# Perceiver cross attention: value products computed transposed, two heads side by side in column halves, then turned back

## What is computed

```
x = x + cross_attention(context, layernorm(x), mask)   # this case's stage
x = x + causal_attention(layernorm(x), Qw, Kw, Vw)
x = x + two_layers_of(local attention + gated FFN)(layernorm(x))

# cross_attention, 16 heads of 64; 4 batches; 256 latents; context of 4096 tokens of width 256
xn, ln_lat = layer_norm(context), layer_norm(latents)
q = ln_lat @ Wq
k, v = split(concat([xn, ln_lat]) @ Wkv)
weight = where(mask, (q * s) @ (k * s).T, -max)        # s = 64 ** -0.25
out = softmax(weight) @ v ; result = out @ Wout
```

## Time and profile before

| | before |
|---|---|
| median of 3 runs | 1054.46 us (1053.11 to 1055.18) |
| the profiled execution | 1054.65 us |
| span from its first to its last instruction | 1052.8 us |
| granted TensorE clock, mean | 0.995 of 2.4 GHz |
| PE / PEld / DVE / ACT / POOL busy | 1014.3 / 943.1 / 809.3 / 666.8 / 204.1 us |

### The profile page before, as it was taken

How to read it: one execution, slowest core, us unless ns; L and a number is a source line. 1 busy time by engine, 2 the same in 40 slices (tenths; PEclk the granted TensorE clock), 3 DMA queues, 4 the chain that set the end, 5 groups by cost and what they waited for, 6 DMA issues and landing times. The chain is left out here.

```text
span 1052.8 us, 25657 instructions
## 1 busy us (share of the span) xinstructions
PE 1014.3 (96%) x8683; PEld 943.1 (90%) x8684; DVE 809.3 (77%) x3001; ACT 666.8 (63%) x1550; POOL 204.1 (19%) x265
## 2 busy tenths in 40 slices
PE   6999999999999999999999998988999999999997
PEld 6899999999999999999999998977888999889887
DVE  7887777685877786787787777579879889889753
ACT  4765565674665665566565566478776876767753
POOL 0111111110111111111111111342015203263213
PEclk9999999999999999999999999999999999999999
DMA  6000000000000000000000100520010000110000
GB/s 208 18 13 2 10 1 1 12 12 4 12 2 0 12 13 3 13 2 0 12 13 2 35 2 2 166 38 2 1 41 21 2 1 21 35 48 2 1 22 21
DMA packets 28803, 21.64 MB, mean 21 GB/s; under 512 B 12094, under 2 KB 26267, under 8 KB 28699
## 3 DMA queue, kind: packets, MB, share of 16 engines
q1 hardware_dynamic: 28529, 20.21, 6.5%
q10 hardware_dynamic: 170, 0.07, 0.0%
HBM read 19.17 MB, written 1.05 MB: 19 GB/s over the span
## 5 line engine op out<-in xcount | busy, mean ns | idle before, releaser
L303 PEld LDWEIGHTS pv_ps<-v,pt 128*128 128x128 f32 x1792 | 214.9, 192 | 9.3 <-issue 2.8
L303 PE MATMUL pv_ps<-v,pt 128*128 128x65 f32 x1792 | 215.2, 272 | 3.2 <-DVE o L818 1.8
L796 DVE CUSTOM_DVE_ANT_0 s_sb<-s_ps,pen,mstate 128x256 f32<-128x256 f32 (+1 forms) x512 | 199.9, 446 | 13.9 <-issue 11.0
L510 ACT ACTIVATE probs<-s_sb,mbias 128x256 f32<-128x256 f32 (+1 forms) x512 | 203.2, 470 | 0.0
L670 POOL TENSOR_TENSOR o<-o,alpha 128x260 f32<-128x260 f32 x128 | 85.7, 669 | 561.3 <-ACT alpha L504 561.3
L519 ACT ACTIVATE pt<-turn 128x512 f32<-128x512 f32 x128 | 76.2, 595 | 123.0 <-PE turn L290 109.1
L290 PE MATMUL turn<-ident,probs 128*128 128x128 f32 x896 | 123.8, 278 | 0.1
L290 PEld LDWEIGHTS turn<-ident,probs 128*128 128x128 f32 x896 | 98.8, 145 | 9.5 <-issue 0.3
L818 DVE TENSOR_TENSOR o<-o,pv_ps 128x260 f32<-128x260 f32 x128 | 53.9, 421 | 46.1 <-PE pv_ps L303 34.7
L279 PE MATMUL s_ps<-kh,qh 64*128 64x256 f32 (+1 forms) x512 | 78.9, 304 | 2.9 <-DVE x L840 1.6
L768 DVE TENSOR_TENSOR kl<-proj,kh 128x512 fp32r<-128x512 f32 (+1 forms) x63 | 41.3, 655 | 51.5 <-ACT kh L497 51.0
(11 more groups left out here) (432 smaller groups left out, 2730.7 us busy)
## 6 DMA issues: line engine op xcount, KB each, us to landing
raw<-in_ctx SPq DMA_DIRECT2D x24, 128.0 KB, 2.0
f_wqkv_raw<-in_L_ffn_wqkv SPq DMA_DIRECT2D x6, 512.0 KB, 5.3
f_w_raw<-in_L_ffn_w SPq DMA_DIRECT2D x8, 256.0 KB, 5.1
f_w_raw<-in_L_ffn_w SPq DMA_DIRECT2D x2, 640.0 KB
wkv_raw<-in_L_xattn_Wkv SPq DMA_DIRECT2D x1, 1024.0 KB, 8.5
wout_raw<-in_L_xattn_Wout SPq DMA_DIRECT2D x1, 1024.0 KB, 12.5
f_wo_raw<-in_L_ffn_wo SPq DMA_DIRECT2D x2, 512.0 KB, 4.7
x<-in_x SPq DMA_DIRECT2D x1, 768.0 KB, 9.6
```

The source lines that it names most:

```text
L303: last = pe.matmul(t.pv_ps[:, u, :], t.pt[g % 2][:, u, kt, :], t.v[:, kt, h, :], start=(kt == 0), stop=(kt == kts - 1))
L510: last = act.activation(t.probs[g % 2][:, u, 0:kts * P], t.s_sb[g % 2][:, u, 0:kts * P], ACT.Exp, bias=t.mbias[:, at:at + 1], scale=0.125)
L796: last = dve.tensor_tensor_reduce(out=t.s_sb[g % 2][:, u, 0:width], in0=t.s_ps[g % 2][:, u, 0:width], in1=t.pen[:, 0:width], scale=1.0, sc ...
```

## The change

`weighted_values` swaps its operands: a head's values (128 keys by 64) are the weights, and the turned probabilities of both query tiles (256 columns) stream past. The first head of a group writes PSUM partitions 0 to 63, the second 64 to 127. The result is the transposed output; it goes into parts of `s_ps[0]`, is copied by ACT (`store_outputs`) into `ov`, turned back on PE (`turn_back`) into `pv_ps`, and added by DVE. Since there is no column of ones any more, the exponentials give their row sums (`accum_out`), and POOL adds them to the denominator. All of it happens for two groups at a time, at odd steps: the products behind the probabilities' transposes (ahead of them in `finish` steps), the turning back behind the projection (directly behind the transposes in `finish` steps).

```diff
+    def pair_at(m, kind, prev, j):
+        return [now for now in (at_step(m, kind, prev, j - 4), at_step(m, kind, prev, j - 3)) if now] if j % 2 else []
+    def output_bank(g):
+        return t.s_ps[0][:, 2 - g % 2 * 2, :]
...
 def weighted_values(m, g, kts):
-                if g or not isinstance(m, int):
-                    pe.wait_ge(s["o_added"], 8 * m + g)
-                for u in range(GU):
-                    h = 2 * g + u // QT
-                    for kt in range(kts):
-                        last = pe.matmul(t.pv_ps[:, u, :], t.pt[g % 2][:, u, kt, :], t.v[:, kt, h, :],
+                for kt in range(kts):
+                    for o, rows in enumerate((slice(0, DH), slice(DH, P))):
+                        last = pe.matmul(output_bank(g)[rows, :], t.v[:, kt, 2 * g + o, :], t.pt[g % 2][:, QT * o:QT * o + QT, kt, :],
                                          start=(kt == 0), stop=(kt == kts - 1))
                 last.then_inc(s["pv_done"], 1)
+            def turn_back(pair):
+                for m, g, kts in pair:
+                    pe.wait_ge(s["ov_stored"], 8 * m + g + 1)
+                first_m, first_g, _ = pair[0]
+                if first_g or not isinstance(first_m, int):
+                    pe.wait_ge(s["o_added"], 8 * first_m + first_g)
+                for m, g, kts in pair:
+                    for qt in range(QT):
+                        last = pe.transpose(t.pv_ps[:, 1 - g % 2, qt * P:(qt + 1) * P], t.ov[g % 2][:, qt * P:(qt + 1) * P], t.ident[:])
+                last.then_inc(s["o_turned_back"], len(pair))
...
 PE body
+                    pair = pair_at(m, kind, prev, j)
+                    if pair and finish:
+                        pe.wait_ge(s["s_read"], 8 * m + (j + 2 if kind else 2))
+                        for now in pair:
+                            weighted_values(*now)
                     now = at_step(m, kind, prev, j - 2)
                     if now:
                         turn_probs(*now)
+                    if pair and not finish:
+                        pe.wait_ge(s["s_read"], 8 * m + (j + 2 if kind else 2))
+                        for now in pair:
+                            weighted_values(*now)
+                    if pair and finish:
+                        turn_back(pair)
...
-                    now = at_step(m, kind, prev, j - 3)
-                    if now:
-                        weighted_values(*now)
+                    if pair and not finish:
+                        turn_back(pair)
...
 ACT
-                                          bias=t.mbias[:, at:at + 1], scale=0.125)
+                                          bias=t.mbias[:, at:at + 1], scale=0.125, accum_out=t.sums[:, at:at + 1])
+            def store_outputs(m, g, kts):
+                act.wait_ge(s["pv_done"], 8 * m + g + 1)
+                if g >= 2 or not isinstance(m, int):
+                    act.wait_ge(s["o_turned_back"], 8 * m + g - 1)
+                act.activation(t.ov[g % 2][:], output_bank(g), ACT.Copy).then_inc(s["ov_stored"], 1)
 ACT body
                 for j in range(NG if kind else 6):
+                    for now in pair_at(m, kind, prev, j):
+                        store_outputs(*now)
...
 POOL body, behind the rescaling of o
+                    pool.wait_ge(s["rescaled"], 16 * m + 2 * g + 1)
+                    pool.wait_ge(s["p_ready"], 8 * m + g + 1)
+                    pool.tensor_tensor(t.o[:, cols, DH], t.o[:, cols, DH], t.sums[:, cols], ALU.add).then_inc(s["rescaled"], 1)
...
 DVE add_output
-                dve.wait_ge(s["pv_done"], 8 * m + g + 1)
-                dve.tensor_tensor(t.o[:, cols, :], t.o[:, cols, :], t.pv_ps[:], ALU.add).then_inc(s["o_added"], 1)
+                added = t.o[:, cols, 0:DH].rearrange("p (o q) d -> p o q d", q=QT)
+                dve.tensor_tensor(added, added, t.pv_ps[:, 1 - g % 2, :].rearrange("p (q o d) -> p o q d", q=QT, o=2), ALU.add
+                                  ).then_inc(s["o_added"], 1)
 DVE body
-                    now = at_step(m, kind, prev, j - 4)
-                    if now:
-                        add_output(*now)
...
                     if now:
                         store_turned(*now)
+                    pair = pair_at(m, kind, prev, j)
+                    if pair:
+                        last_m, last_g, _ = pair[-1]
+                        dve.wait_ge(s["o_turned_back"], 8 * last_m + last_g + 1)
+                        for now in pair:
+                            add_output(*now)
```

## The result

| | before | after |
|---|---|---|
| median | 1054.76 us (1053.11 to 1055.18) | 1082.5 us (1080.5 to 1082.5) |
| span of the profiled execution | 1052.8 us | 1080.3 us |
| granted TensorE clock, mean | 0.995 | 0.989 |

After over before is 1.026, with a 95% interval of 1.024 to 1.028. The change is slower by 27.7 us; the forecast was a gain of 24. The range of 1008 to 1088 held the time, but the sign was wrong. A fourth run of the kernel after, at a granted clock of 0.749, took 1226.1 us and is left out of its column.

The account below looks back on a forecast made before the run. PE's own work was taken to bound the cross stage, so 1054.65 - 35.9 of PE work + 12.3 of new waits gave 1031 us, bounds 998 to 1044. The range over most rivals was 1008 to 1088.

Parts of the forecast that it names:

- PE's work: Cross stage: products 110.4, division changes 21.1 and turning back 25.6 added, 193.0 removed; sum -35.9 us.
- The overlap: Value products: the two heads run at once in the two column halves; the rival without overlap, 1113 us, had chance 0.2.
- the hidden weight loads: Value products: loads overlap earlier products, slots stay 0.215 us; the rival of uncovered loads, 1059 to 1087 us, had chance 0.1.
- the order of the slots: Value products in program order, A1, then A2 beside B1, and so on: a full pair takes 9 slots, 1.94 us.
- Below 110 there is nothing: Lower bound of the value products' total, 110 us, because each half has its own eight passes in a row.
- the sum of the bounds: Fast end of the forecast's bounds: 1054.65 - 35.9 - 21 - 12, given as 998 us.
- the tokens' wait: Step 3: the tokens' transposes wait for `proj` from ACT, 0.42 us open in 15 bodies, 6.3 us.
- the 12.3 us of new waits: PE's added waits: tokens 6.3, halves 2.4, finishing bodies 3.6, ordinary turning back nothing; bounds 0 and 25 us.
- about 0.8 us to spare: Odd steps: after DVE's wait for the turning back, PE and DVE meet their next duty with about 0.8 us left.
- another engine's chain: Rival: ACT, or DVE behind its new wait, half a microsecond late at each of 64 pairs; +32 us, 1063 us, chance 0.12.
- Half, step 5: No projection stands between a half's products and the turning back: 0.6 us of wait, four times, 2.4 us.
- Finishing steps: Three finishing bodies: only transposes cover ACT's copy, which has others queued; 0 to 0.6 us, taken as 0.3, for 12 pairs.

Follow-up runs that it names:

- e10: e3 with both heads' products in the same half of the columns, so the second head's output is wrong and unused; 1167.92 us, ratio 1.107.
- e3: The changed kernel with a group's two product loops exchanged: both key tiles of the first head, then both of the second; 1082.33 us, ratio 1.0249.
- e1: The changed kernel with DVE's additions of a pair put off behind maxima and store_turned of the next even step; 1068.83 us, ratio 1.013.
- e12: e9 with the change's own products, transposed in column halves and turned back, in the halves (one key tile) too; 1059.24 us, ratio 1.0031.
- e7: The changed kernel with DVE's store_turned (copy of the turned probabilities) ahead of maxima in every step; 1071.21 us, ratio 1.0142.
- e6: The changed kernel with add_result (x) ahead of keys_lo in steps 6 and 7 of the finishing passages; 1076.4 us, ratio 1.02.
- e9: The changed kernel with old products in halves, not waiting for scores' readers; additions put off inside plain bodies, x before keys_lo, penalties behind last maxima; 1041.41 us, ratio 0.9872.
- e13: The changed kernel with twelve unused identity transposes ahead of PE's waits for x at step 7 of finishing passages and the next pair; 1083.92 us, ratio 1.0264.

## Why the prediction was wrong

**Right in kind, and the near number is partly luck: PE's work.** -34.8 us of busy time against -35.9. The full pair was forecast at 1.94 us and a change of the array's division at 0.33 us a visit. Measured are 1.88 us with the way out of it, and 0.22 us ahead of it (eight transposes from 300.68 to 301.70 take 1.02, in the earlier trace rows 0.80). Together 2.10 against 2.27 us. Turning back was forecast at 0.10 us a transpose: four take 0.52 us, of which 0.10 is the way into the scores' division that was there before. So by distances of starts a full pair takes 2.52 us where it took 3.46: 0.94 saved instead of 0.79, some 45 us instead of 38 in 48 pairs. The busy time shows less, because PE worked at a lower clock for longer (some 5 us), and because the record of the last matmul ahead of a wait reaches past the start of the next one: the projection's last record runs from 300.21 to 300.49, the next would have started at 300.33. At some 50 more waits than before such ends make up the rest, by my estimate.

The overlap (e10) and the hidden weight loads (both passes of a slot start together every 0.215 us, which is the columns' time) went as taken. The Trainium skill, in "TensorE: Matmul & The Clock Gate", Part 3, The mechanism, has the rule that weight loads overlap products in flight only when the row groups differ, though its first lines also let a load go ahead through a background weight buffer. The rule as it stands doesn't hold for these products, which share all row groups: their slots are 0.215 us in after, in e3 and, with both heads in one half, in e10.

**Near total, wrong step: the order of the slots.** The nine slots of a pair came from a rule about program order. There are eight, and e3 shows that program order does not decide. "Below 110 there is nothing" is wrong with it: 48 pairs of eight slots and 16 of four are 96 us.

**Wrong in the sum of the bounds.** 1054.65 - 35.9 - 21 - 12 is 986, not 998. The 998 comes out with no wait at all, so without the last term.

**Right: the tokens' wait.** 0.42 us in 15 bodies, 6.3 us; measured 6.1 us, 14 times. ACT's reads at 0.09 us were right as well (306.30 to 306.39), and no wait of PE names POOL.

**Wrong, the step that decided: the 12.3 us of new waits, and in it "about 0.8 us to spare" on DVE.** PE's idle time grew by 62.3 us. I took DVE's wait for the turning back for harmless because it ends where PE starts the next scores, and looked only at the *products'* need of turned probabilities. Missed was that `turn_probs` itself waits for the copies out of its own two banks, and that the copy stands behind the next maxima. DVE in order of time in the kernel after, for the 1.27 us at 311.05:

```profile
305.84 0.75 DVE L862 TENSOR_TENSOR o<-o,pv_ps 128x256 f32<-128x256 f32 x2 [1.28 <-PE pv_ps L321]
306.51 0.68 DVE L812 TENSOR_TENSOR kl<-proj,kh 128x512 fp32r<-128x512 f32 x1
...
308.02 0.06 DVE L837 MEMSET tick<- 128x1 f32 x1 [0.63 <-ACT probs L543]
...
310.30 0.69 DVE L856 COPY pt<-turn 128x512 f32<-128x512 f32 x1
```

Idle 1.28 us for the turning back; then the additions 0.67, `kl` 0.60, penalties to 307.39, 0.63 us of standing still, maxima 2.2, and only then the copy that PE's next transposes need. The 0.63 us are not ACT's, though the row names it: by the code these maxima need the exponentials of group 6, which were done at 303.2. This is where a body ends, and the trace has records of DVE's sequencer there (the loop's branch and register work, L145, from 307.13 on), which the views do not print. The kernel before has 0.57 us at its body's end (ahead of 299.75). From the start of the additions (305.84) to the end of the copy (310.99) it is 5.2 us, while PE, had it not waited, would have been back at its transposes at 309.78 (311.05 less 1.27), 3.9 us on. There was no room, and the rows of before could have told. Over the cross stage 20 waits of 0.75 us on average came to 15.0 us.

But the additions are not the link that decides here. In e1 they are gone from this place, and PE's transposes still wait. DVE, then PE, in order of time in e1:

```profile
300.68 0.69 DVE L812 TENSOR_TENSOR kl<-proj,kh 128x512 fp32r<-128x512 f32 x1 [1.35 <-ACT kh L530]
...
302.65 0.06 DVE L837 MEMSET tick<- 128x1 f32 x1 [0.69 <-PE s_ps L287]
```
```profile
305.68 1.09 PE L298 MATMUL turn<-ident,probs 128*128 128x128 f32 x8 [1.17 <-DVE pt L856]
```

Instead of the turning back DVE waits for ACT's copy of the keys, and the penalties and the body's end stand behind that. The maxima start 2.27 us behind PE's scores (300.38), in after 2.38 (behind 305.64), in before 1.23 (298.90), where the value products stood between the projection and the scores and covered the keys' way. With the penalties moved away as well, in e12, they start 1.29 us behind them (295.25), and the transposes' wait is 0.16 us. With the copy ahead of the maxima, in e7, it is nothing. So inside plain bodies the transposes were late because the copy stood behind the maxima, and these behind the penalties and the keys' way. The place of the additions alone changed little there; its 13.7 us lay elsewhere, mostly in the passages with finishing steps.

The rival "another engine's chain" named the mechanism, at 0.12 and 32 us; waits of this sort (`pt` from DVE and ACT, `mnew`) come to 22.5 us. It should have been the likeliest case, since an average of 83% busy says nothing of the order within a step.

**Wrong: the covers that the removed work had given.** The value products had stood at the end of every step. I listed what they covered for the tokens, and stopped there. They covered the way from the projection over ACT's `kh` and DVE's `kl` as well, the 1.35 us of e1 among them: in the finishing steps x stood behind it (11.3 us, e6), and behind step 7 the next queries (4.6 us). Those 16 us were not in the sum.

**Wrong in size: ACT in half and finishing steps.** Half, step 5: taken as 0.6 us, measured 1.21. Finishing steps: taken as 0.3 us for each of 12 pairs, 3.6 us; together `ov` cost 12.7 us in 14 waits. ACT has the even step's exponentials, or in a finishing step a whole group's, ahead of the copy; with one key tile PE's products are over in 1 us and cover none of it.

**Not in the prediction: the clock.** A new idle time of PE can be followed by a fall of its clock, here 5 us in all.

## What to carry to other kernels

When work leaves a saturated engine, list everything that it stood in front of: each wait behind it on that engine loses the cover, and here 62 us of new idle time stand against 35 us less of busy time. An engine's new wait must be followed through its own queue to each later consumer, including the buffer that the first engine wants back, by adding up one step's rows and not by its busy share. Then try the rows on paper again with that wait taken away: if the next releaser ends as late, as ACT's copy of the keys did behind DVE's additions, the first one is not the cause. Such a change pays where its hand-overs are covered and not where they are bare (bodies with one key tile). The same idea went from +2.6% to +0.3% by DVE's order alone (e12), and to -1.3% with the old products kept in the bodies with one key tile (e9).

## What the runs showed of the hardware

- fp32 products into different column halves, with 64-column weights and the same 128 input partitions, start two at a time every 0.215 us, eight slots for sixteen passes, whatever their order in the program (1.88 and 1.92 us). In the same half they run one by one (3.59 us).
- Going in and out of the column halves costs 0.22 and some 0.16 us (1.88 less 8 x 0.215).
- A read of ACT's accumulator has a record of 190 ns, but the next operation starts 0.09 us behind it; 512 of them made 41.5 us of ACT's time.
- In the cross stage, falls of the granted clock (a mean of 0.66 in 5 us, or as much spread over two such stretches) came behind idle times of PE of 1.2 to 2.2 us in after, e9 and e13, but not behind each of them; a us of lost clock went with 0.68 us of time.
- At a body's end DVE stood still for 0.57 us in before and 0.63 in after, with its sequencer's loop records in that time; a row can name another engine for such time.
